# Attention and expert FFN in fp32 on one core: key and query rows stacked four partitions apart, the second norm folded into centred weights, new orders

## What is computed

```
Q = layernorm(x) @ Wq.T + bq;  K = ctx @ Wk.T + bk;  V = ctx @ Wv.T + bv
x = x + softmax(Q K^T / 4) V @ Wo.T + bo            # 16 heads, 256 x 256 scores each
y = layernorm(x)
scores = softmax(y @ G);  w = the two largest scores of each token, zero elsewhere
h = silu(y @ gate) * (y @ up);  lr = y @ lora_A     # 8 experts side by side
x = x + (h * w) @ down + (lr * w) @ lora_B
```

## Time and profile before

| | |
|---|---|
| time, median of 3 runs | 154.72 us (154.31 to 155.24) |
| span of the profiled execution | 150.3 us; its own time is not given apart from the runs |
| PE busy | 123.6 us (82%), 936 instructions |
| DVE busy | 93.0 us (62%), 189 instructions |
| ACT busy | 68.7 us (46%) |
| POOL busy | 49.3 us (33%) |
| mean granted clock of PE | 0.909 of full speed |
| moved by the DMA rings | 11.92 MB, 4.34 MB of it read from HBM |

### The profile page before, as it was taken

The page is one execution under the profiler, slowest core; times in us unless marked ns, Lnnn a source line. Parts: engine busy times, 40 slices in busy tenths (PEclk is TensorE's granted clock), DMA queues, the critical chain, the costliest instruction groups (busy, mean ns, idle before and its releaser), DMA issues.

```text
span 150.3 us, 2628 instructions
## 1 busy us (share of the span) xinstructions
PE 123.6 (82%) x936; PEld 94.6 (63%) x936; DVE 93.0 (62%) x189; ACT 68.7 (46%) x116; POOL 49.3 (33%) x76
## 2 busy tenths in 40 slices
PE   5998661928998586499998499998999999999980
PEld 5996451928886463366574258755667578788760
DVE  4451606006498969238799569999859535866801
ACT  3116540241164243658937431989596731415110
POOL 7978602064052109800007030253500750250000
PEclk9999996595599879659999869999999999999999
DMA  4931699999999992000999100000000002002022
GB/s 133 258 133 38 144 128 187 122 156 134 171 240 142 146 255 40 2 4 4 156 122 124 20 0 4 0 4 2 7 0 0 0 4 70 0 0 74 0 74 70
DMA packets 9181, 11.92 MB, mean 79 GB/s; under 512 B 1296, under 2 KB 5712, under 8 KB 9168
## 3 DMA queue, kind: packets, MB, share of 16 engines
q1 hardware_dynamic: 8128, 10.56, 39.8%
q10 hardware_dynamic: 1040, 1.18, 4.6%
HBM read 4.34 MB, written 1.05 MB: 36 GB/s over the span
## 4 chain that ended last, share of the span: by engine, by line
PE 61%; DMA 13%; issue 7%; DVE 5%; SPq 4%; POOL 4%; ACT 3%; ACTq 0%; POOLq 0%; DVEq 0%
PE unit L719 23%; DMA qstack<-q_lo 8%; PE unit L832 7%; PE unit L800 7%; PE unit L726 5%; DMA kstack<-k_lo 5%; PE unit L819 5%; SPq L311 4%; PE unit L841 4%; PE unit L739 3%; PE unit L875 2%; POOL wf_lo L450 2%; PE unit L877 2%; PE unit L876 2%; DVE rowmax L644 1%
## 5 line engine op out<-in xcount | busy, mean ns | idle before, releaser
L644 DVE TENSOR_REDUCE rowmax<-unit 128x4 f32<-128x1024 f32 x32 | 37.7, 1214 | 18.6 <-PE unit L800 18.6
L549 ACT ACTIVATE probs<-unit 128x1024 f32<-128x1024 f32 x32 | 31.5, 1024 | 15.2 <-PE unit L819 9.8
L800 PE MATMUL unit<-kstack,qstack 48*128 48x256 f32 x128 | 16.0, 358 | 9.5 <-DMA qstack<-q_lo 3.3
L800 PEld LDWEIGHTS unit<-kstack,qstack 48*128 48x128 f32 x128 | 11.2, 227 | 15.7 <-issue 9.8
L426 POOL TENSOR_SCALAR vare<-mv 128x2 f32<-128x2 f32 x8 | 1.8, 223 | 52.2 <-DVE mv L591 52.1
L832 PE MATMUL unit<-probs,vaug 128*32 128x256 f32 x256 | 17.9, 409 | 0.0
L819 PE MATMUL unit<-qstack,kstack 49*128 49x256 f32 x128 | 13.7, 318 | 1.4 <-DVE rowmax L644 0.9
L819 PEld LDWEIGHTS unit<-qstack,kstack 49*128 49x128 f32 x128 | 10.1, 202 | 5.8 <-issue 2.9
L588 DVE BATCH_NORM_STATS2 stats<-xs 128x6 f32<-128x256 f32 x16 | 6.0, 418 | 9.9 <-DMA xs<-x 9.7
L832 PEld LDWEIGHTS unit<-probs,vaug 128*32 128x32 f32 x256 | 7.3, 115 | 6.3 <-issue 2.5
L719 PE MATMUL unit<-wf_hi,xT_hi 128*128 128x256 f32 (+1 forms) x32 | 9.4, 374 | 0.5 <-POOL xT_lo L441 0.5
(11 more groups left out here) (108 smaller groups left out, 241.6 us busy)
## 6 DMA issues: line engine op xcount, KB each, us to landing
kstack<-k_hi SPq DMA_DIRECT2D x16, 128.0 KB, 9.1
qstack<-q_hi SPq DMA_DIRECT2D x12, 128.0 KB, 8.2
xs<-x SPq DMA_DIRECT2D x4, 256.0 KB, 6.4
kstack<-k_lo SPq DMA_DIRECT2D x8, 128.0 KB, 10.8
out<-res SPq DMA_DIRECT2D x4, 256.0 KB, 2.2
probs<-wattn SPq DMA_DIRECT2D x3, 256.0 KB, 6.8
cT<-ctxT SPq DMA_DIRECT2D x3, 256.0 KB, 7.0
qstack<-q_lo SPq DMA_DIRECT2D x6, 128.0 KB, 7.0
```

The lines of the kernel that those rows point to most:

```text
L549: act.activation(probs[:, n % NPAIR], unit[PAIR[name, n] // 2][:], ACT.Exp, scale=SCALE).then_inc(exp_done, 1)
L644: dve.tensor_reduce(rowmax[:, b % 2, :, :, i].rearrange("p t j -> p j t"), unit[PAIR[name, n] // 2][:], AX.X, ALU.max)\
L800: ins = pe.matmul(dst[:, j, t], qs[rows, i, t * P:(t + 1) * P], ks[rows, i], start=True, stop=True)
```

## The change

- **Stacks.** A head pair's parts now lie four partitions apart: row 4i+g holds part g of row i, g from 0 to 2, and rows 3, 7, ... hold the edge: 0 in `qstack` (with the maxima at rows 63 and 127), -1 in `kstack`. A part is stacked with one transfer of 128 source and 32 target partitions (256 KB), six for a batch in place of twelve. The products read all 64 rows of a half. Batch 0's stacks are prepared by two memsets, the edge rows of the stacks of batches 1 and 2 by four transfers (`fillk`, `fillq`) from a small tile `edge`, those of batch 3's queries by a short one. The row of maxima goes out in one transfer instead of two.
- **Raw operands.** `wk`, `wq`, `wv`, `wf` and all four batches of `cT` have tiles of their own; `probs` has six buffers. `q` is a raw fp32 product in every batch, k and v only in batch 0; `low` in every batch, with 136 columns; `glu` raw in batch 3.
- **Second norm.** x2 is turned round as it is. `mean` and `mlow` average the FFN weights over the features, `wfc` and `wlc` subtract that from them, so that the mean of x2 falls away; the reciprocal root comes in as the scale of the tanh (`half_rstd`) and through `weight_low` and `weight_hid`.
- **Sums in place.** x with the bias, x2 and the result all stand in `xs`, which is stored from there; hid and low are weighted in place.
- **Orders.** New lists for all engines, ten warm-up products instead of 24, and one semaphore for each stage name and engine.

```diff
-WHOLE = {("k", 0), ("q", 0), ("v", 0)}
...
+NPAIR = 6
+NVALUE = 3
...
+KV_PARTS = (1, 2, 3)
+GLU_PARTS = (0, 1, 2)
+LOW_BY_VECTOR = (0,)
+NORM_BY_VECTOR = (0,)
+WEIGHED_BY_GPSIMD = (0, 1, 2)
...
-        v:0@0 k:0@1 xT:0@0 q:0@0 xT:1@1 k:1@0 q:1@1 k:2@0 v:1@1 max:0.0@2 max:0.1@4 max:0.2@6 xT:2@0 v:2@1
-        max:0.3@2 max:0.4@4 q:2@0 max:0.5@6 v:3@1 max:0.6@2 k:3@0 max:0.7@4 max:1.0@6 max:1.1@2 xT:3@0
-        max:1.2@6 max:1.3@4 mrow:0@0 q:3@0 max:1.4@2 max:1.5@6 max:1.6@4 bias:0@0 max:1.7@2 attn:0.0@6
...
+        k:0@0 xT:0@1 bias@2 q:0@1 mean@0 k:1@2 xT:1@3 v:1@4 max:0.0@0 max:0.1@6 q:1@3 max:0.2@4 max:0.3@0 xT:2@2
+        k:2@6 max:0.4@4 max:0.5@2 q:2@7 max:0.6@0 max:0.7@4 v:0@6 max:1.0@0 xT:3@2 max:1.1@4 max:1.2@6 mrow:0@3
+        q:3@2 max:1.3@0 max:1.4@4 v:2@3 attn:0.0@6 max:1.5@0 attn:0.1@2 max:1.6@4 attn:0.2@6 max:2.0@0 attn:0.3@2
+        attn:0.4@4 max:1.7@6 max:2.1@0 attn:0.5@2 max:2.2@4 mrow:1@6 u:0.0@7 attn:0.6@0 max:2.3@2 u:0.1@7
...
-        x:0 wv x:1 wk c:1 wq c:2 khi:0 x:2 c:3 klo:0 khi:1 qhi:1 x:3 klo:1 outs qlo:1 khi:2 qhi:2 wf klo:2
-        mstack:0 qlo:2 mstack:1 qhi:3 khi:3 qlo:3 klo:3 mstack:2 mstack:3 out:0 out:1 out:2 out:3
...
+        x:0 wk wv x:1 fillq:2 wo x:2 fillq:1 x:3 c:2 fillk:1 ks0:0 wd ks1:0 qs0:0 qs1:0 c:3 fillk:2 ks0:1 ks1:1
+        qs0:1 qs1:1 qs0:2 ks1:2 ks0:2 ms:0 qs1:2 ms:1 fillq:3 qs0:3 qs1:3 ks0:3 ks1:3 ms:2 ms:3 out:0 out:1 out:2
+        out:3
...
-        wa = flat_probs[:, 0:KT * WA].rearrange("p (k o) -> p k o", k=KT)
-        wf = flat_probs[:, KT * WA:KT * (WA + WF)].rearrange("p (k o) -> p k o", k=KT)
...
+        def part_rows(stack, g):
+            return stack[g:P:4].bitcast(F32).rearrange("i (q k) t -> i q (k t)", k=KT)
...
-        def stack_rows(engine, stack, parts, g, j, stacked):
-            lo = HALF * j + HD * g
-            engine.dma_start(stack[lo:lo + HD].bitcast(F32).rearrange("r (q k) t -> r q (k t)", k=KT),
-                             parts[HALF * j:HALF * (j + 1)].bitcast(F32).rearrange("p k t -> p (k t)")).then_inc(stacked, 16)
...
+                if name == "fillk":
+                    wait(sp, "edge")
+                    sp.dma_start(kstack[b][3:P:4].bitcast(F32),
+                                 edge[:, 0].bitcast(F32).unsqueeze(1).to_broadcast([QUAD, PAIRS, T])).then_inc(k_stacked[b], 16)
+                if name == "fillq":
+                    wait(sp, "edge")
+                    if b < NSTACK:
+                        sp.dma_start(qstack[b][3:P:4].bitcast(F32),
+                                     edge[:, 1].bitcast(F32).unsqueeze(1).to_broadcast([QUAD, PAIRS, S]))\
+                            .then_inc(q_stacked[b], 16)
+                    else:
+                        wait(sp, "attn", b - NSTACK, PAIRS - 1)
+                        sp.dma_start(qstack[b][HALF - 1:P:HALF].bitcast(F32),
+                                     edge[0:2, 1].bitcast(F32).unsqueeze(1).to_broadcast([2, PAIRS, S]))\
+                            .then_inc(q_stacked[b], 16)
...
+                if name == "ms":
+                    wait(sp, "mrE", b)
+                    wait_stacked(sp, "q", b)
+                    sp.dma_start(qstack[b][HALF - 1:P:HALF].bitcast(F32),
+                                 mT[:, b % 2].bitcast(F32)).then_inc(m_stacked[b], 16)
...
-                    if n == 0:
-
-                        act.wait_ge(wa_lo_ready, len(LO_TURN))
-                        act.wait_ge(wf_ready, 1)
...
+                    act.activation(hid[:, b % 2, i], work[BANK["glu", b, i]][:, 0], ACT.Tanh, scale=half_rstd[:, b, i:i + 1])\
+                        .then_inc(done["th"], 1)
...
+                if name == "wfc":
+                    wait(dve, "mean")
+                    for k in range(KT):
+                        ins = dve.tensor_tensor(wf[:, k, 0:2 * EF], wf[:, k, 0:2 * EF],
+                                                work[BANK["mean", 0, 0]].rearrange("p o f -> p (o f)"), ALU.subtract)
+                    ins.then_inc(done["wfc"], 1)
...
+                    link(dve.tensor_tensor(below[:], logit, wide(top[:]), ALU.subtract))
+                    wait(dve, "rs2", b)
+                    dve.tensor_tensor(below[:], below[:], wide(rstd[:, 1, b]), ALU.mult).then_inc(done["r1"], 1)
...
+                if name == "res":
+                    wait(dve, "down", b)
+                    dve.tensor_tensor(xs[:, b], work[BANK["down", b, 0]], xs[:, b], ALU.add).then_inc(done["res"], 1)
...
-                            rows = slice(HALF * j, HALF * j + ROWS)
-                            ins = pe.matmul(dst[:, j, t], qs[rows, i, t * P:(t + 1) * P], ks[rows, i],
+                            rows = slice(HALF * j, HALF * (j + 1))
+                            ins = pe.matmul(pair[:, j, t], qstack[b][rows, i, t * P:(t + 1) * P], kstack[b][rows, i],
...
+                if name == "mean":
+                    wait(pe, "ones")
+                    pe.wait_ge(wf_in, 16)
+                    for k in range(KT):
+                        ins = pe.matmul(dst.rearrange("p o f -> p (o f)"), mean[:], wf[:, k, 0:2 * EF],
+                                        start=(k == 0), stop=(k == KT - 1))
+                    ins.then_inc(done["mean"], 1)
...
+                if name == "q":
+                    pe.wait_ge(wq_in, 16)
+                    wait(pe, "xTE", b)
+                    for o in range(KT):
+                        ins = product(dst[:, o], lambda _, k: wq[:, k, o * P:(o + 1) * P], lambda _, k: xT[:, b % 2, k], ((0, 0),))
+                    ins.then_inc(done["q"], 1)
...
+                if name == "low":
+                    wait(pe, "wlc")
+                    wait(pe, "x2w", b)
+                    for t in range(ST):
+                        ins = product(dst[:, t, 0:LOW], lambda _, k: x2T[:, b % 2, k, t * P:(t + 1) * P],
+                                      lambda _, k: wf[:, k, 2 * EF:], ((0, 0),))
...
+                if name == "glu":
+                    rows = slice(i * P, (i + 1) * P)
+                    if b in GLU_PARTS:
+                        wait(pe, "wfl")
+                        wait(pe, "x2lo", b)
+                        ins = product(dst.rearrange("p o f -> p (o f)"), lambda p, k: (x2T_hi, x2T_lo)[p][:, k, rows],
+                                      lambda p, k: (wf_hi, wf_lo)[p][:, k], PARTS)
```

More of the change, by code:

```diff
@@ new lines, in wait, with wait_evacuated @@
+        def wait(engine, name, b=0, i=0):
+            engine.wait_ge(raised[ON[name, b, i]][name], TURN[name, b, i])
+        def wait_evacuated(engine, name, b, i):
+            if name in ("k", "q"):
+                wait(engine, f"{name}lo" if b in LOW_BY_VECTOR else f"{name}w", b)
+            if name in ("v", "xT"):
+                wait(engine, f"{name}E", b)
+            if name == "max":
+                wait(engine, "mx", b, i)
+            if name == "mrow":
+                wait(engine, "mrE", b)
+            if name == "attn":
+                wait(engine, "e", b, i)
+            if name == "u":
+                wait(engine, "uT", b, i // 2)
+            if name == "o":
+                wait(engine, "x2", b)
+            if name == "x2T":
+                wait(engine, "x2w", b)
+            if name == "low":
+                wait(engine, "lowE", b)
+            if name == "glu":
+                wait(engine, "h", b, i)
+            if name in ("hT", "lT"):
+                wait(engine, f"{name}E", b)
+            if name == "down":
+                wait(engine, "res", b)
+            if name == "bias":
+                wait(engine, "bp")
+            if name == "mean":
+                wait(engine, "wfc")
+            if name == "mlow":
+                wait(engine, "wlc")
@@ L400, in _ @@
         def _(pool):
+            done = raised["gpsimd"]
             chain = [0]
@@ new lines, in _ @@
+                if name in ("khi", "qhi", "kw", "qw"):
+                    of = name[0]
+                    hi, whole, bias = (k_hi, k_whole, bk_sb) if of == "k" else (q_hi, q_whole, bq_sb)
+                    dst = hi[:, b % 2] if name[1:] == "hi" else whole
+                    wait(act, of, b)
+                    if b == 0:
+                        act.wait_ge(bias_in, 16)
+                    if name[1:] == "hi" and b >= 2:
+                        wait_stacked(act, of, b - 2)
+                    if name[1:] == "w" and b - 1 not in LOW_BY_VECTOR:
+                        wait(act, of + "lo", b - 1)
+                    for o in range(KT):
+                        ins = act.activation(dst[:, o], work[BANK[of, b, 0]][:, o], ACT.Identity, bias=bias[:, o:o + 1])
+                    ins.then_inc(done[name], 1)
@@ L566, in _ @@
[L566 to L574 removed]
+                        wait(act, "down", b - 1)
@@ L620, in _ @@
                                                 ALU.subtract, ALU.mult)
-                    ins.then_inc(xn_ready[w], 1)
-                if name in ("xT", "x2T"):
-                    w = int(name == "x2T")
```

(25 more changed lines are left out.)

1015 lines of the change are left out of this document (461 added, 554 removed).

## The result

The changed kernel takes **125.35 us** (median of four runs, 124.76 to 126.23) where the kernel before took 154.84 beside it: a ratio of 0.817, 95% interval 0.808 to 0.826 (here and below the ratio is of executions in the faster of the chip's two states alone; the two medians give 0.810, inside the interval). A second session with six runs gave 125.87, ratio 0.820 (0.816 to 0.824).

A forecast was written before the change was run, and what follows sets the result against it. Three stages bound it: transfers to the first score product (29.2 us), DVE reductions to 62.1, then PE from 60.3 to 129.0. With a 3.7 us tail the span is 132.7, plus 4.4 around it 137.1 us, range 129 to 149.

The forecast's parts named there:

- Transfers until the first score product: First stage: 6.43 MB through the rings at 240 GB/s put the first score product at 29.2 us, bounds 24 and 35.1.
- Stacks gain nothing: Rival on the stacking transfers: fills and stacks go at 150 GB/s, batch 2's stacks 8.7 us late, 145.8 us; chance 0.13.
- Reductions: Middle stage: DVE's row maxima bound the kernel from first score product to batch 2's last maximum, 29.2 to 62.1 us.
- The wait at 39: Reductions stage: DVE waits 1.4 us near 39 for batch 1's stacked rows, q:1 having run at half clock.
- PE to the end: Last stage from attn:1.3: 64.6 us of TensorE work plus 4.1 added, 60.3 to 129.0, then a 3.7 us tail.
- The 4.1 us: Last stage: waits and slow clock of the kernel before (61.6 taken, 57.5 priced), added to PE's work.
- The norm: Last stage: x2's norm leaves ACT, DVE and the way to x2T; costed at nothing since PE had other work.
- The time around the span: Whole kernel: 4.4 us outside the span (4.0 to 4.9), added to the forecast span of 132.7.
- Faster still: Rival: rings at 312 GB/s (5.2 us less) and the 4.1 us of waits gone, 127.8 us; chance 0.15.
- Turn-taking: Rival on maxima and exponentials: three engines wait in turn, DVE at 0.69 stretches 17.7 us to 25.5, 144.9; chance 0.15.
- the DVE bound: Rival on the last stage: DVE's 51.5 us at share 0.71 take 72, giving 142.0 us; chance 0.10.
- The slower case: Rival at batch 2's stacks: new fills hold up the queue, 113 GB/s for a full ring, 158.4 us; chance 0.05.

The follow-up runs named there:

- a_first: Changed kernel with bias product, wo load and mean product moved later, c:1 split earlier on POOL and v:1 ahead of xT:1: 125.27 us, ratio 0.814.
- a_halves: Changed kernel, rows still four partitions apart, but each part stacked in two transfers of 64 source to 16 target partitions: 130.36 us, ratio 0.852.
- a_adjacent: Changed kernel with a part's 16 rows adjacent again, each part in two transfers of 64 to 16 partitions: 152.31 us, ratio 0.992.
- b_stack4: Kernel before with stack rows four partitions apart, one transfer of 128 to 32 partitions per part, orders kept: 134.66 us, ratio 0.871.
- b_tiles: Kernel before with the raw attention and FFN weights in tiles of their own: 150.73 us, ratio 0.972.
- b_both: Kernel before with both own tiles for the raw weights and stack rows four partitions apart: 131.96 us, ratio 0.852.
- a_adj0: Changed kernel with the old form of the stacking transfers in batch 0 alone: 134.33 us, ratio 0.873.
- a_first2: a_first with x:3's moments moved behind the third pair of maxima and the bias sum ahead of that pair: 123.81 us, ratio 0.806.

## Why the prediction was right in sign and wrong in size

Against the profiled execution (126.23) the sum is 10.9 us too long: 4.4 until attn:1.3 (60.3 forecast, 55.9 measured), 3.5 from there to the last product of PE, 0.4 in the tail, 2.6 around the span.

- **Transfers until the first score product: the rate was mis-sized.** "I take 240" was the failed step. It put the first score product at 29.2, and it came at 24.4, 4.8 us earlier. The 240 was the rate of rings that had a quarter of their share free; I used it for a queue that I had just said to have no pause. In the changed kernel loads and the first fills moved 283 at a share of 0.88 in the same window, loads, fills and stacks together 344 at 0.94, and the queue as a whole 350 for the time its rings were busy. Even at the 312 of my upper bound the queue ahead (5.4 MB) is through at 19.7 and no longer binds. What is left to the transfers is what I gave as the lower end, last issue (20.5 forecast, 21.4 measured) plus a short landing: rows in by 23.9. PE's own list, behind its wait for wo, comes 0.5 us later and sets the 24.37; a_first, with the list turned, has the product at 19.4. The page on port swizzle that I took for the sign alone ranks the forms as measured. By its rule (Trainium skill, SBUF — State Buffer, "Door 1: The DMA port swizzle") 16 adjacent rows reach 4 ports, 16 rows four apart in one half 8, and 32 rows over both halves 16. The runs agree in order: 350 GB/s for the last, 321 for the middle one (11.23 MB in 0.267 x 131.2 us), 184 for the first, mixed with loads.
- **Stacks gain nothing (145.8 as a rival): under-priced.** With slow stacks the changed kernel takes 152.3, of which 5.0 go with the split of each transfer in two (a_halves). I had counted bytes up to batch 2's stacks, 8.7 us, and nothing behind them. The row of maxima behind those stacks (8.02 us for 16 KB) and batch 3's keys (5.3 us of wait) were missing; I named both and hid both under other work. Missing too was what a wait does to PE's clock: 7.4 us more of busy time in a_adjacent, 8.2 less in b_stack4 than before.
- **Reductions: right.** 32.9 us forecast from first product to last maximum of batch 2, 34.06 measured (24.37 to 58.43); DVE is busy 29.54 of 32 us. The wait at 39 did not come: q:1 ran at full clock (1.92 us, where I had 3.5 at half), and PE fed the maxima in pairs between its own products. Nor did PE ever wait for a row of maxima, so the 2 us that I named for it are not in the time. The first exponential came at 41.4, 17.0 behind the first product, where I had 16.3. The wait for POOL is gone as forecast, but by b_tiles and b_both the tiles bring only 2.7 to 4.2 us; the form alone already moves the first attention product from 58.0 to 45.7.
- **PE to the end: the carried waits failed.** I priced the work at 64.6, and that was right: from attn:1.3 at 55.86 to 121.10 PE is busy for 64.36 of 65.24 us. Raw gate products cost 1.72 and not 2.0, low 1.12 against 1.05. The 4.1 us "which I add" became 0.9, the wait for hidT, with the clock at 1.00. A sum of old waits was carried into a list written without them. This is the second term that failed, 3.2 us of it.
- **The norm: right by accident.** I costed it at nothing because PE had other work. In the old orders that is near (1.1). In the new ones there is 0.9 us of it between o and x2T, and the step costs 12.5 to 19.8; the fold is what lets the list stand as it does.
- **The time around the span.** I set one execution's span (150.3) against the median of other runs and got 4.4. Both numbers of one execution show 1.8 us for the changed kernel (126.23 with 124.4) and 1.7 to 3.2 for the kernel before (154.84 with 153.1, 152.96 with 150.1, 154.87 with 151.7 in a later session). By these the profiled execution took 152.0 to 153.5 us, less than the median.
- **Rivals.** "Faster still", 127.8, had both of its terms come true (rings over 312, waits all but gone) and I gave it 0.15; the rest of the miss is the time around the span. Turn-taking and the DVE bound did not show: DVE 0.77 and PE 0.99 in the last stage. The slower case's rate of 113 is not far from what the old form shows in the new kernel (116 GB/s at share 1.04, 112 for a full ring, from 50 to 58 of a_adjacent), but the new form never comes near it.

Apart, on the kernel before: form and number of the transfers 20.2 us, own tiles 2.7 more, and 6.6 for all the rest, new orders with the fold above all. Each part is the difference to the step before it, so that they sum to the 29.5 proves nothing.

## What to carry to other kernels

Price a slow transfer at every place that waits for its queue, small transfers behind it included: undoing the form in batch 0 cost 9 us, in all batches 27 (5 of them with the doubled number). Price PE's clock behind a long wait as well: in a_adj0 it made 5.1 us into 8.0, and about half of what the new form gave the kernel before was PE's products running faster (8.2 of the 16.9 us between the profiled spans). A rate read at a share under 1 is not the rate of a full queue; divide by the share first. For a form that the trace doesn't show, forecast with both ends worked through to the time; the end at which the resource stops binding is a case of its own, not the edge of a range. A wait read in the old kernel belongs to the old order; before carrying it over, look in the new order for what stands between producer and consumer. And take span and time from the same execution.

## What the runs showed of the hardware

- Where the rows of a transfer between tiles of the on-chip memory land decides its rate: the same 12 transfers a batch of 128 KB with 64 source partitions took 4.9 to 6.1 us in the median onto 16 adjacent partitions and 2.3 to 2.9 onto 16 partitions four apart. A window of the slow form alone shows 116 GB/s at a DMA share of 1.04:

```profile
50.00:58.00 8.00, 4.60 (x27) 3.53 (x25) 3.26 (x3) 2.15 (x5) 3.94 (x3) 0.88 1.04 116
```

- One queue issues a transfer every 0.6 us (ten in a row from 33.87 to 40.16 in a_halves), and that shows: 12 transfers a batch in place of 6, at 321 GB/s, cost 5 us all told; in the chain of waits it is the row of maxima that stands behind the issues.
- In the changed kernel the granted clock had fallen to the lower level (1.2 GHz; 0.50 from 13.6 to 19.2 us) when PE's wait of 4.95 us ended at 13.68, and the raw product behind took 3.41 us for 1.97. In a_adj0 it was 0.53 over 29.4 to 36.2 us, behind a wait of 5.47. Short waits don't settle it: in a_first2, with waits of 2.0 us at most, the mean over the span was 1.00 in the profiled execution and 0.972 to 0.999 in the others, and in a_first, with 1.6 at most, the clock was at 0.50 from 12.4 to 15.5 us.
